# VectorE's small operands moved to a PSUM bank and its routing steps reordered, in an attention and mixture-of-experts kernel on one core

## The reference

```python
n = layernorm(x)                       # no affine part, eps 1e-5
q, k = n @ Wq / 4, n @ Wk              # 16 heads of 16 features
v = n @ Wv                             # 16 heads of 8 features
# per head, causal: weight of key s for query t is (q_t . k_s)^2, s <= t
o_t = sum_s (q_t.k_s)^2 v_s / (sum_s (q_t.k_s)^2 + 1e-5)
x = x + o @ Wo
n = layernorm(x)
score = softmax(n @ gate_w + gate_b)   # 8 experts
# each token goes to its two best; of these the one with the higher number gives the result
x = x + relu(n * score_e @ w1[e] + b1[e]) @ w2[e] + b2[e]
```

## Time and profile before

| | |
|---|---|
| median of 3 runs | 286.66 us (285.38 to 289.38) |
| profiled execution | 289.88 us |
| its span in the trace | 288.20 us |
| busy: TensorE, VectorE, ScalarE, GpSimd | 252.2, 202.7, 168.5, 172.9 us |
| mean granted clock of TensorE | 0.911 of full speed |

### The profile page before, as it was taken

How to read it: one execution, slowest core, us unless ns; L and a number is a source line. 1 busy time by engine, 2 the same in 40 slices (tenths; PEclk the granted TensorE clock), 3 DMA queues, 4 the chain that set the end, 5 groups by cost and what they waited for, 6 DMA issues and landing times.

```text
span 288.2 us, 9383 instructions
## 1 busy us (share of the span) xinstructions
PE 252.2 (88%) x3254; PEld 203.5 (71%) x3254; DVE 202.7 (70%) x709; ACT 168.5 (58%) x319; POOL 172.9 (60%) x178
## 2 busy tenths in 40 slices
PE   5877999979969969987997997677899999999993
PEld 2655677656746756765676675554698999999993
DVE  4535556896897789689689879777888855555552
ACT  2235787566764855756676667543564556556540
POOL 6241764565694595778577477593157776445455
PEclk9657999968986995996898999997999999999999
DMA  5799999999500000000000000007685669767510
GB/s 141 211 280 299 358 359 357 356 346 342 170 19 2 21 21 0 22 2 22 20 3 19 12 13 21 21 21 187 175 231 166 159 179 295 208 193 196 142 35 12
DMA packets 31711, 40.61 MB, mean 141 GB/s; under 512 B 3587, under 2 KB 24485, under 8 KB 31665
## 3 DMA queue, kind: packets, MB, share of 16 engines
q1 hardware_dynamic: 29392, 35.76, 41.7%
q0 software_dynamic: 2272, 4.25, 4.3%
HBM read 17.98 MB, written 22.48 MB: 140 GB/s over the span
## 4 chain that ended last, share of the span: by engine, by line
PE 52%; DVE 31%; issue 7%; POOL 5%; ACT 4%; DVEq 0%; POOLq 0%; ACTq 0%
PE sc L1151 20%; PE av L1151 17%; PE p L1151 13%; DVE scaled L824 4%; DVE logit L826 3%; ACT scores L444 2%; PE p L1154 2%; POOL rstd L626 2%; DVE p L774 2%; DVE stats L802 2%; DVE shift L741 2%; DVE rows L794 1%; DVE oT L790 1%; DVE stats L698 1%; DVE o_sb L785 1%
## 5 line engine op out<-in xcount | busy, mean ns | idle before, releaser
L611 POOL TENSOR_TENSOR scores<-scores,causal 128x768 f32<-128x768 f32 (+1 forms) x48 | 78.2, 1634 | 38.6 <-ACT scores L444 38.4
L444 ACT ACTIVATE scores<-sc 128x1792 f32<-128x1792 f32 (+1 forms) x48 | 76.3, 1590 | 33.6 <-PE sc L1151 32.5
L1151 PE MATMUL sc<-q_sb,k_sb 32*128 32x128 f32 (+3 forms) x1024 | 58.6, 356 | 18.2 <-ACT scores L444 15.4
L1151 PEld LDWEIGHTS sc<-q_sb,k_sb 32*128 32x128 f32 x1024 | 46.0, 203 | 37.2 <-issue 29.1
L654 POOL DMA_INDIRECT out<-y_sb,xr x39 | 38.4, 986 | 26.6 <-DVE y_sb L1091 20.6
L555 ACT ACTIVATE hT<-sc,b_sb 128x128 f32<-128x128 f32 x78 | 24.5, 363 | 32.4 <-PE sc L1151 31.6
L1151 PE MATMUL sc<-xwT,w_t 128*128 128x128 f32 x312 | 41.4, 276 | 0.0
L1151 PE MATMUL av<-scores,v_ext 128*32 128x256 f32 (+3 forms) x1024 | 40.1, 310 | 0.6 <-DVE raw L796 0.6
L637 POOL DMA_INDIRECT expert_rows<-rows,slot_i x32 | 32.3, 1008 | 11.5 <-issue 7.2
L1079 DVE TENSOR_SCALAR hT<-sc,b_sb 128x128 f32<-128x128 f32 x78 | 23.9, 346 | 21.2 <-PE sc L1151 17.8
L1151 PEld LDWEIGHTS sc<-xwT,w_t 128*128 128x128 f32 x312 | 38.0, 192 | 0.0
(11 more groups left out here) (159 smaller groups left out, 377.7 us busy)
## 6 DMA issues: line engine op xcount, KB each, us to landing
expert_rows<-pad_rows SPq DMA_DIRECT2D x11, 1572.0 KB, 18.0
w_t<-in_L_ffn_w SPq DMA_DIRECT2D x39, 256.0 KB, 3.2
xr<-expert_rows SPq DMA_DIRECT2D x39, 65.5 KB, 2.9
rows<-in_L_attn_hidden_states SPq DMA_DIRECT2D x16, 128.0 KB, 2.7
out<-y_sb,xr POOLq DMA_INDIRECT x39, 3.3
b_sb<-in_L_ffn_b SPq DMA_DIRECT2D x1, 512.0 KB, 6.5
expert_rows<-rows,slot_i POOLq DMA_INDIRECT x32, 2.4
wk_sb<-in_L_attn_Wk SPq DMA_DIRECT2D x1, 128.0 KB, 2.6
```

Of the source, the lines that this page charges most:

```text
L444: nc.scalar.activation(unit(b, u)[:, :, :], sc[:, :, 0:WIDTH[u]], ACT.Square, scale=Q_SCALE).then_inc(squared, 1)
L611: nc.gpsimd.tensor_tensor(own, own, not_after(own), ALU.mult).then_inc(masked, 1)
L1151: return nc.tensor.matmul(o, lhsT=l, rhs=r, start=start, stop=stop)
```

## The change

**Operands.** The bank `p7` no longer holds the spread result, which goes to SBUF (`u_sb`). In its place the bank holds the small tensors of VectorE's chains: `den`, `rden`, and by the class `Small` raw, scaled, logit, rank, gap, rsum, score, key, place, taken and factor. Each instruction with two tensor inputs of these chains has one input there and one in SBUF. For that a copy of the logits (`logit_s`), of the first norm's roots (`rstd_p`) and of the factor is added. Pairs 6 and 7 use an SBUF tensor of the same layout (`late_small`).

**Order on VectorE.** In a period: `gate_x`, `residual`, `norm2_stats`, `part_k`, `norm1_scales`, `norm1_stats` of one batch in each period, the choice steps up to `route_place`, `spread`, `divide`, then `route_taken` and `route_rows`, then the logits steps.

**The other queues.** ScalarE's `exponent` moves to the next period, behind `square(core, 0)`. GpSimd's `norm1_root` moves from odd periods to the even one before it is used, its `norm2_root` behind `mask(core, 0)`; `scatter` runs one period later, so that period 16 holds two of them. TensorE's `prefix` moves behind `weigh`.

The layout, the lags and ScalarE's queue:

```diff
-        den = sb("den", [P, NG * L // STRIP, 2])
-        rden = sb("rden", [P, NG * L // STRIP, 2])
+        u_sb = sb("u_sb", [P, L // STRIP, NG, 2, SUB])
...
-        u_ps = p7[:, :].rearrange("p (n g r w) -> p n g r w", n=L // STRIP, g=NG, r=2)
 
         def output_bank(b):
             return projected[0 if b < NB - TAIL else 1]
+
+
+        den, rden = [p7[:, 32 * i:32 * (i + 1)].rearrange("p (n r) -> p n r", r=2) for i in range(2)]
+
+        rstd_p = p7[:, 440:440 + PAIR * NTK].rearrange("p (b j) -> p b j", b=PAIR)
...
+                self.raw = place(PAIR, NTK, E)
+                self.scaled = place(PT, E)
+                self.logit = place(PT, E)
+                self.rank = place(PT, E)
+                n = PT * E * E
+                self.gap = place(PT, E, E)
+                at -= n
+                self.rsum = bank[:, at:at + PT]
+                at += PT
+                self.score, self.key, self.place = [
+                    bank[:, at + PT * E * i:at + PT * E * (i + 1)].rearrange("p (j e) -> p j e", j=PT) for i in range(3)]
+                at += 3 * PT * E
+                self.taken = bank[:, at:at + 2 * PT].rearrange("p (n j) -> p n j", n=2)
+                at += 2 * PT
+                self.factor = bank[:, at:at + PT].rearrange("p (b j) -> p b j", b=PAIR)
+
+        smalls = [Small(p7), Small(late_small)]
+
+        def small(k):
+            return smalls[0 if k < EARLY else 1]
...
-        CORE, LATE, TAIL, LOGITS, CHOICE, SEND = 1, 2, 3, 4, 5, 5
+        CORE, LATE, TAIL, LOGITS, CHOICE, SEND = 1, 2, 3, 4, 5, 6
...
-                logits = pair_of(p, LOGITS)
+                choice = pair_of(p, CHOICE)
...
                 square(core, 0)
+                if choice is not None:
+                    exponent(choice)
...
-                if logits is not None and p < NB:
-                    exponent(logits)
```

GpSimd's queue, the chains (the routing steps not shown are changed in the same way) and the order on VectorE and TensorE:

```diff
-                if logits is not None and p < NB:
-                    norm2_root(logits)
-                if roots1 is not None and roots1 > 2:
-                    norm1_root(ln1_count(PAIR * roots1), slice(PAIR * roots1, PAIR * roots1 + PAIR))
+                if pair_of(p, -2) is not None and p > PAIR:
+                    norm1_root(p + 2, slice(p + 2, p + 2 + PAIR))
                 mask(core, 0)
                 if p == NB:
+                    scatter(send + 1)
+                if p == 1:
+                    norm1_root(PAIR, slice(PAIR, 2 * PAIR))
+                if logits is not None:
                     norm2_root(logits)
+                mask(core, 1)
                 if p == 1:
-                    norm1_root(ln1_count(PAIR), slice(PAIR, 2 * PAIR))
-                mask(core, 1)
-                if roots1 == 2:
-                    norm1_root(ln1_count(2 * PAIR), slice(2 * PAIR, 3 * PAIR))
+                    norm1_root(2 * PAIR, slice(2 * PAIR, 3 * PAIR))
                 if send is not None and p < NB:
                     scatter(send)
                 mask(core, 2)
...
-                nc.vector.scalar_tensor_tensor(out=shift1[:, at, :], in0=mv1[:, at, :, 0], scalar=-1.0, in1=rstd1[:, at, :],
+                nc.vector.tensor_copy(rstd_p, rstd1[:, at, :]).then_inc(ln1_copied, 1)
+                dve.wait_ge(ln1_copied, b // PAIR - 1)
+                nc.vector.scalar_tensor_tensor(out=shift1[:, at, :], in0=mv1[:, at, :, 0], scalar=-1.0, in1=rstd_p,
                                                op0=ALU.mult, op1=ALU.mult).then_inc(x_scaled, 1)
-                nc.vector.tensor_tensor(std1[:, at, :], ve1[:, at, :], rstd1[:, at, :], ALU.mult)
+                nc.vector.tensor_tensor(std1[:, at, :], ve1[:, at, :], rstd_p, ALU.mult)
...
-                nc.vector.transpose(u_ps.rearrange("p n g r w -> p g n (r w)"),
+                nc.vector.transpose(u_sb[:, :, :, :, :].rearrange("p n g r w -> p g n (r w)"),
...
-                nc.vector.tensor_scalar_add(den[:, :, :], heads[:, :, :, HD], ATT_EPS).then_inc(den_step, 1)
+                heads = u_sb[:, :, :, :, :].rearrange("p n g r w -> p (n g) r w")
+                nc.vector.tensor_scalar_add(den, heads[:, :, :, HD], ATT_EPS).then_inc(den_step, 1)
                 dve.wait_ge(den_step, 3 * b + 1)
-                nc.vector.reciprocal(rden[:, :, :], den[:, :, :]).then_inc(den_step, 1)
+                nc.vector.reciprocal(rden, den).then_inc(den_step, 1)
                 dve.wait_ge(den_step, 3 * b + 2)
                 nc.vector.tensor_tensor(o_sb[:, :, :, :, :].rearrange("p n g r d -> p (n g) r d"), heads[:, :, :, 0:HD],
-                                        rden[:, :, :].unsqueeze(3).broadcast_to([P, NG * L // STRIP, 2, HD]),
+                                        rden.unsqueeze(3).broadcast_to([P, NG * L // STRIP, 2, HD]),
...
                 dve.wait_ge(ln2_rstd, k + 1)
-                then(1, nc.vector.tensor_tensor(scaled[:, :, :], of_pair(raw, k).rearrange("p b j e -> p (b j) e"),
+                then(1, nc.vector.tensor_tensor(t.scaled, t.raw.rearrange("p b j e -> p (b j) e"),
                                                 wide(flat(of_pair(rstd2, k))), ALU.mult))
-                then(2, nc.vector.tensor_tensor(logit[:, :, :], scaled[:, :, :], shared(gb_sb[:, :]), ALU.add))
-                then(3, nc.vector.reduce_max(top[:, :], logit[:, :, :], AX.X))
+                then(2, nc.vector.tensor_tensor(t.logit, t.scaled, shared(gb_sb[:, :]), ALU.add))
+                nc.vector.tensor_copy(logit_s[:, :, :], t.logit)
+                then(3, nc.vector.reduce_max(top[:, :], t.logit, AX.X))
 
                 after(dve, expo_ready, k)
-                nc.vector.tensor_tensor(shifted[:, :, :], logit[:, :, :], wide(top[:, :]),
+                nc.vector.tensor_tensor(shifted[:, :, :], t.logit, wide(top[:, :]),
                                         ALU.subtract).then_inc(shifted_ready, 1)
...
+                t = small(k)
+                then(4, nc.vector.tensor_tensor(t.gap, t.logit.unsqueeze(2).broadcast_to([P, PT, E, E]),
+                                                logit_s[:, :, :].unsqueeze(3).broadcast_to([P, PT, E, E]), ALU.subtract))
+                then(5, nc.vector.tensor_tensor(ahead[:, :, :, :], t.gap,
...
-                if choice is not None:
-                    route_sum(choice)
-                    route_score(choice)
-                    route_onehot(choice)
-                if pair_of(p, -2) is not None:
-                    norm1_scales(p + 2)
-                if stats is not None:
-                    norm1_stats((PAIR * stats, PAIR * stats + 1), ln1_count(PAIR * stats))
                 if tail is not None:
                     residual(tail)
                     norm2_stats(tail)
@@ -1052,21 +1082,26 @@
                     table_done(first, 0, tile_row)
                 if new is not None:
                     part_k(new)
+                if pair_of(p, -2) is not None:
+                    norm1_scales(p + 2)
+                if p + 4 < NB:
+                    norm1_stats((p + 4,), ln1_stats_count(p + 4))
                 if choice is not None:
+                    route_sum(choice)
+                    route_score(choice)
+                    route_onehot(choice)
                     route_place(choice)
-                    route_taken(choice)
-                    route_rows(choice)
-                if logits is not None and p < NB:
-                    if logits == 0:
-                        dve.wait_ge(bias_in, 16)
-                    route_logits(logits)
-                    route_ahead(logits)
-                    route_best(logits)
                 if late is not None:
                     spread(late)
                     divide(late)
                 if p == NB:
                     first_left(first)
+                if choice is not None:
+                    route_taken(choice)
+                    route_rows(choice)
+                if logits is not None:
+                    if logits == 0:
+                        dve.wait_ge(bias_in, 16)
                     route_logits(logits)
                     route_ahead(logits)
                     route_best(logits)
@@ -1335,10 +1370,10 @@
                 if p == NB:
                     weigh(late)
                 score(core, 1)
+                if p < NB:
+                    weigh(late)
                 if choice is not None:
                     prefix(choice)
-                if p < NB:
-                    weigh(late)
                 score(core, 2)
                 if new is not None:
```

More of the change, by code:

```diff
@@ L153, in attention_moe_kernel @@
         raw_x = sb("raw_x", [P, NB, NTK, E])
-        raw = sb("raw", [P, NB, NTK, E])
-        scaled = sb("scaled", [P, PT, E])
-        logit = sb("logit", [P, PT, E])
+        late_small = sb("late_small", [P, 512])
+        logit_s = sb("logit_s", [P, PT, E])
         top = sb("top", [P, PT])
@@ L650, in _ @@
             for b in range(PAIR):
-                norm1_root(b + 1, slice(b, b + 1))
+                norm1_root(b, slice(b, b + 1))
             def send_result(t):
```

(14 more changed lines are left out.)

53 lines of the change are left out of this document (28 added, 25 removed).

## The result

The changed kernel took 264.59 us (median of 4 runs, 261.21 to 266.98) where the kernel before, run beside it, took 287.38 (285.38 to 289.38). All ratios in this document leave out executions more than 1.5% above the shortest one of the same kernel on the same chip; here these are two of the changed kernel's four and none of the kernel before. The plain medians give 0.921, and 264.59 is 1.6 above the low end. The profiled execution took 266.98 us, with a span of 265.3, and is 2.4 above its own median.

What follows compares the result with a forecast made beforehand. Bound: mask-delayed VectorE chains idling TensorE, then half clock, in periods 4 to 15. From the profiled 289.88 us, -23.3 (115.8 against 139.1) and +2.4 for the passage gave 269.0; range 263 to 278.

Steps and rivals of the forecast that it cites:

- What bounds the kernel: Routing periods 4 to 15: masks stretch VectorE instructions with two SBUF inputs, TensorE idles, half clock follows; 29 us reachable.
- Operands: VectorE's small instructions in the routing periods: a PSUM destination adds 0 to 30 ns each, taken as 0 in the sum.
- The rival at 274: VectorE's chains become the bound if PSUM operands cost 60 ns more: +0.8 a pair, 5 in all; chance 0.12.
- the one by which the masks hold up PSUM operands too: Rival: GpSimd's masks still delay `onehot` and the logits, 1.6 us a pair, ten in all, 279; chance 0.04.
- Even period: Period with the logits steps: `exponent` gone from in front of the last square, so it lasts 9.15 us.
- Odd 10.25: Period with the choice steps: the moved logits chain and `prefix` behind `weigh` make it last 10.25 us.
- Both reasons given for the longer odd period: Logits chain delays `gate_x` to 1.8 to 2.2 us instead of 0.6; `prefix`, waiting for `onehot`, holds TensorE 0.5.
- the rival at 279: Half clock stays in the odd periods because `project_k` and `prefix` still wait: +9 to +11 us; chance 0.13.
- The slower rival: Late `norm2_root` or last mask holds up `gate_x`, TensorE idles: 25.4 us a pair, about 303; chance 0.03.
- Passage: Period 16 into the expert stage: pair 6's SBUF operands wait for two masks, +2.4 us, bounds 0 and +3.5.
- the forecast's own sign of being wrong: At the passage: the prediction is wrong if the expert stage's start absorbs the delay, forecast at +2.4 us.
- I do not take 3.2 off: Whole kernel: the sum keeps the profiled execution's 3.2 us above the median, since the new schedule has no half-clock periods to lose.

Runs made afterwards that it cites:

- f2: Kernel before with its old order, only the small tensors moved to PSUM: 260.08 us, ratio 0.923 to the kernel before.
- f5: Changed kernel with pair 6's small tensors also in PSUM and the choice steps ahead of the first norm's statistics: 263.65 us, ratio 0.923 to before.
- g2: f5 with the ranking moved across the period boundary, behind `gate_x`: 259.31 us, ratio 0.908 to the kernel before.
- e1: Changed kernel with its new order but all small tensors in SBUF: 317.99 us, where the kernel before took 305.38.
- f1: e1 run again on another chip, new order with small tensors in SBUF: 299.49 us, ratio 1.060 to the kernel before.
- f0_changed_again: The changed kernel itself, unaltered, run again on another chip: 266.01 us, ratio 0.941 to the kernel before.
- g0: f2 run once more, unchanged: 260.17 us (257.73 to 264.5).
- g1: f2 with pair 6's small tensors in PSUM as well: 262.65 us, ratio 0.919 to the kernel before.
- second and third group: Two later sets of follow-up runs, each read against the kernel before, which took 285.19 us in one and 287.15 in the other.
- the first group: First set of follow-up runs, cutting the change in two, on a chip where the kernel before took 305.38 us.
- e3: Changed kernel with pair 6's small tensors in PSUM as well: 301.38 us, one execution, where the kernel before took 305.38.

## Why the prediction was right and wrong

**What bounds the kernel.** Right, and shown: `scaled`, `logit`, `picked`, `onehot` were stretched by masks; the order of before with nothing but other operands (f2) has even periods of 9.14 and full clock, and ScalarE waits 0.3 us for `shifted` in periods 4 to 15 and 2.3 in period 16, where it waited 19.3 us in seven waits before. The Trainium skill's rule (SBUF — State Buffer, "SBUF: two separate sides") is that a Vector instruction with two SBUF inputs and a GpSimd instruction that reads SBUF exclude each other. The traces agree on both sides: 0.19 us for `best` inside a mask with its input in PSUM, 1.42 in SBUF.

**Operands.** Forecast 0 to 30 ns each, measured at most 25. The rival at 274 by dearer PSUM operands falls, and so does the one by which the masks hold up PSUM operands too.

**Order.** Even period forecast 9.15, measured 9.14. Odd 10.25, measured 10.11; the last pair's 9.65 was 9.77. Periods 4 to 15 forecast 115.8, measured 114.8. The difference lies in the odd periods: period 5 took 9.84, and period 13, which the forecast counted with statistics that it does not have (p + 4 is past the last batch), 9.76. `gate_x` was laid out at 1.8, measured 1.80; `onehot` 6.95, measured 6.61; the wait of `prefix` 0.5, measured 0.28. Both reasons given for the longer odd period were tested one by one: the choice behind the statistics is worth 0.35 (f5), the ranking in front of `gate_x` 0.39 (g2).

What the forecast never asked is what the order buys. It summed both halves as one, which hid that the second half is a loss: the total of 139.1 - 114.8 = 24.3 would have been 26 without it. The expectation for the order alone (e1) named the mechanism, a mask that holds up a logits step in front of `gate_x`, but put the odd period at 11 to 11.5 where f1 shows 14.4: two steps meet a mask there, not one (`shifted` 2.08, `best` 1.42), and TensorE, idle for 3.31 us, works on at half clock.

**Clock.** No odd period fell to half clock; the rival at 279 falls. f1 shows the half clock behind an idle stretch of 3.31 us (granted clock 0.88 over that period). The slower rival's mechanism, a chain in front of `gate_x` that makes TensorE idle in every pair, is what f1 is: 9.77 + 14.4 = 24.2 a pair (forecast for the rival 25.4; its sum, 289.9 + 13 + 2, is 305 and not 303). It came by the masks, not by `norm2_root`, and the operands in PSUM keep it away.

**Passage.** Forecast +2.4 at `spread(15)`, measured +2.0 (16.8 for 14.8) by the steps named, `scaled` and `logit` behind two masks. f5, with these in PSUM, halves it (15.9), g2 removes it (14.4). It does not reach the expert stage at its start, as the forecast had it, and by the forecast's own sign of being wrong this counts against it: the first `go_up` comes only 0.4 later than before (16.6 for 16.2). It does so at `prefix(6)`, +2.0, and from period 16 to the end it is +1.7 (103.2 for 101.5).

**The step that failed** is "I do not take 3.2 off". The sum is against the profiled execution, and for that it holds: 269.0 forecast, 266.98 measured, the 2.0 made up of 1.0 in periods 4 to 15, 0.4 before period 4 and 0.6 from period 16 on. But the median is 264.59. The forecast argued that an execution of before can be shorter by fewer odd periods at half clock, of which the new schedule has none to lose. The changed kernel, at full clock in all odd periods, has the same spread: 2.4 between profile and median, 261.21 to 266.98 in all. Two executions of the same instructions show where it lies. The timeline of after:

```profile
18.79 2.07 PE L1186 MATMUL p<-xnT,wq_sb 128*128 128x256 f32 x4
20.79 1.23 PE L1186 MATMUL p<-wv_sb,xnT 128*64 128x72 f32 x16
21.95 1.88 PE L1186 MATMUL sc<-q_sb,k_sb 32*128 32x256 f32 x24
```

and of `f0_changed_again`:

```profile
16.14 1.13 PE L1186 MATMUL p<-xnT,wq_sb 128*128 128x256 f32 x4
17.20 0.72 PE L1186 MATMUL p<-wv_sb,xnT 128*64 128x72 f32 x16
17.86 1.16 PE L1186 MATMUL sc<-q_sb,k_sb 32*128 32x256 f32 x24
```

The same four matmuls take 2.07 us in one and 1.13 in the other, and period 2 starts at 28.97 or 24.43. That is half and full clock. It is read from the rows: in `before` rows of this length (17.60, 2.08 us) stand in a stretch whose granted clock is 0.51. The traces of `after` and f5 have no clock entry so early, so their windows print 1.00 there. The stretch up to period 2 in `before`, `after`, f0 and g0, and that piece of `before`:

```profile
0.00:29.36 29.36, 21.63 (x135) 14.22 (x135) 13.11 (x71) 10.72 (x16) 10.94 (x36) 0.71 0.81 235
0.00:28.97 28.97, 21.28 (x135) 13.78 (x135) 12.80 (x70) 10.73 (x16) 9.66 (x33) 1.00 0.84 253
0.00:24.43 24.43, 16.46 (x135) 10.86 (x136) 12.74 (x70) 10.71 (x16) 9.64 (x33) 0.93 0.80 227
0.00:23.15 23.15, 14.66 (x136) 9.48 (x136) 13.24 (x70) 10.74 (x16) 9.66 (x33) 1.00 0.78 221
...
16.00:22.70 6.70, 6.69 (x60) 5.01 (x60) 2.04 (x13) 2.77 (x4) 2.53 (x3) 0.51 0.93 250
```

TensorE is busy 4.8 us longer in `after` than in f0 with the same matmuls, and period 2 comes 4.5 later. Both profiled executions that the forecast joins, of before and after, had the late start (29.36, 28.97). The four profiled executions that start late (before, after, f5, g1) lie 3.2, 2.4, 2.2 and 0.1 above the median of their kernel, the four that start early (f0, f2, g2, g0) 1.2, 0.1, 1.9 and 2.4 below it. The start is outside the change, so what it adds to one execution above the median belonged off the sum: at most 269.0 - 3.2 = 265.8, 1.2 from the median. Of the 7.1 us between 269.0 and the 261.9 that the ratio gives, this is 3.2; the sum's own terms are 2.0, and 2.0 lie between the ratio 0.914 and that of the plain medians, 0.921. The trace had these rows: the earlier trace rows begin at period 3, and the first 29 us, where the variable part stands, are in none of the groups. The range lacks the same term.

What stays open: why the start falls to half clock in some executions; and period 5, which takes 9.84 in after and 11.54 in f0, with a hole of 1.30 us in TensorE at 58.79 for which the trace names only "issue" (no releaser in the profile). It partly cancels the early start, but does not go with it (f5 and g1 have it with a late start, g2 lacks it with an early one). The DMA records of the traces give a hint that no run tests: in the five with a hole of 1.0 to 1.5 us in period 5 (f0, f2, f5, g0, g1) a 16 KB transfer of instructions starts 4.9 to 5.3 us into the period, and the hole begins within 0.3 us of its end; in after and g2 that transfer starts at 3.6 to 3.7 and there is no hole. How much of before's own 3.2 is start can't be told, since it has one profile. Fewer half-clock periods can be part of it, as the forecast said: in the 15 other executions of before in the second and third group the mean granted clock is 0.907 to 0.969, in all but one above the profiled one's 0.911, and the five shortest (281.42 to 283.18 us) have 0.942 to 0.969.

## What to carry to other kernels

If small VectorE instructions grow to the length of GpSimd's, move one input of each to PSUM first and measure that alone: here it gave 8 to 9% (6% on the chip of the first group) and the reordering that came with it took 2% back. Do not let a chain cross a period's boundary in front of the instruction that frees TensorE's bank; put the short freeing instruction first and the chain behind it (g2: 0.4 us an odd period). And before anchoring a forecast to one profiled execution, read the stretch outside the change for half-clock rows: what varies there belongs in the step from the profile to the median, and in the range.

## What the runs showed of the hardware that was not expected

- `shifted` at 127.69 in f1 began 0.19 us ahead of the mask at 127.88 and ended with it, 2.08 us later; in e1 one began 0.54 us ahead of its mask (101.71, 102.25) and ended with it too, though alone it takes 0.19. So the recorded starts do not tell which of the two instructions waits. Both times GpSimd's `scatter` was still under way when `shifted` began, and what held it first is not shown.
- On one chip the kernel before took 305.38 us and in the other groups 285.19 to 287.38. There a square began 1.7 us after its scores were complete (e3), which no trace of the other chips shows, and the share of the gain was smaller (f2's kernel 0.941 there, 0.923 on the chip of the second group). The cause is open.
- TensorE reaches period 2 between 23.2 and 29.3 us, and the same kernel at 28.97 or 24.43 (after, f0), 25.66 or 23.15 (f2, g0), which is more than the effect of most single edits here; cutting the traces at a fixed instruction gave differences of 0.1 to 0.4 us where medians of 4 runs could not.
